# Graph attention, 16 batches on one core: two bodies per loop turn, another table of units for the next batch's transposes, and SyncE's loads by unit

## The chip, the cores and the metric

One NeuronCore of one Trainium2 chip runs the whole program. The metric is the device time of one execution in microseconds (us), the median of several runs. Lower is better.

## The reference

`x` is 16 batches of 1024 rows by 512 columns, `adj` a 1024 by 1024 matrix of zeros and ones, shared by all batches. Per batch:

```python
h = relu(layernorm(x))                        # over the 512 columns, eps 1e-5
q, k, v = h @ Wq + bq, h @ Wk + bk, h @ Wv + bv   # 8 heads of 64 columns
scores = q @ k.T / sqrt(64) + where(adj == 0, -1e9, 0)
x = x + softmax(scores) @ v
```

All of it is float32.

## The kernel before

**Engines.** TensorE (PE) multiplies and transposes. ScalarE (ACT) takes exponentials and evacuates PSUM into the rounded high parts of a number. VectorE (DVE) adds the mask with a running minimum and makes the low parts. GpSimd (POOL) normalises x, makes the low parts of k and v and finishes the output. SyncE (SP) issues every DMA. Each engine has a program of its own, written out by hand, and semaphores tie them together.

**Units.** A batch is 128 units (`UNITS`). There are 8 heads, each head has two groups of four blocks of 128 queries, and each group has 8 units, one per block of 128 keys. In unit u TensorE does, in `body`: `contract_hi` of unit u-2 (O += V times the high part of the transposed probabilities), `turn_probs` (four transposes of 128x128 probabilities into T, which has two banks), `contract_lo` of unit u-2 and, in even units, `score_ahead` (four score matmuls of 128x512 for a block five ahead). ScalarE copies T to `pT` (`probs_hi`), VectorE makes the rest (`probs_low`), and both go through the scores of every second unit (`exponential`, `shift`). In units 2, 10, 18, ... TensorE also turns the group's output back through the bank `misc` (`turn_out`), ScalarE copies it out (`copy_y`), and POOL adds it to x in three operations (`finish`).

**Fills.** All other work of TensorE is put behind certain units by tables, and all of it goes through the one PSUM bank `misc`:

- `QK_SLOTS`: the projections of q and k of the next pair of heads, in units 3, 4, 5, 6, 8, 9, 11 and 12 of each 32 (the last of them for the third pair is in unit 76).
- `V_SLOTS`: the projection of v, in units 121 to 127 and 0, 1.
- `HT_SLOTS`: `turn_h`, four transposes of one of the next batch's eight x tiles, in units 83, 85, 87, 88, 91, 92, 95 and 96. ScalarE makes the high part (`h_high`) in that unit, VectorE the low part (`h_low`) at the start of the next. POOL normalises tile t two units ahead of its slot (`NORM_AT`).
- `STATS_SLOTS`: `stats`, VectorE's mean and variance of the next batch's x tiles, in units 5, 7, 13, 37, 39, 45, 69 and 71.

The function `before` finds who used the bank `misc` last, and each user waits for that one's evacuation.

**SyncE.** x tiles come through `xln`, which holds two tiles (`XLN = 2`): tile t goes to place t % 2 as soon as the tile before it there is no longer needed. Each tile is loaded twice, once for the statistics and once to be normalised. SyncE's list for each quarter of a batch (a pair of heads p, 32 units) is: loads of x for the statistics; wait for the last pair's output, store it, wait for an earlier store and load the next residual (`xres`); copy half 0 of k (`copy_k`, which waits for `k_low`, POOL's low part); further loads for the statistics; copy half 1 of k; the next weights (`load_wqk`, 1 MB). In the third quarter tiles 0 and 1 are loaded between the two halves of k, and tiles 2 to 7 at the end, behind the weights:

```python
                        sp.wait_ge(qk_mm, 4 * (PAIRS * b + p + 1) + 4)
                        load_wqk((p + 2) % PAIRS)
                    if p == len(STATS_SLOTS) - 1 and not last:
                        for t in range(XLN, NB):
                            sp.wait_ge(h_turned, NB * (b + 1) + t - XLN + 1)
                            load_xln(b + 1, t)
```

SyncE takes its list in order, and a wait holds back all that stands behind it.

**The loop.** On each engine batch 0 and batch 15 are written out as they are, and batches 1 to 14 are one body in a loop (`Fori(1, B - 1)`), so each engine goes back to the top of its loop 13 times. The waits of the body count with the loop's register.

Of the kernel before, what the change touches and what calls it, by code (L numbers as in the profile page):

```python
# [34 lines left out]
B, N, D, H = 16, 1024, 512, 8  # L35
HD = D // H
C = D // P
NB = N // P
PAIRS = H // 2
GROUPS = 2 * H  # L40
GB = NB // 2
UNITS = GROUPS * NB
# [21 lines left out]
HIGH_AFTER = (1, 2)  # L64
LOW_AFTER = (1, 3)

HT_SLOTS = (83, 85, 87, 88, 91, 92, 95, 96)
HT_AT = {s: t for t, s in enumerate(HT_SLOTS)}
NORM_AT = {s - 2: t for t, s in enumerate(HT_SLOTS)}

STATS_SLOTS = ((5, 7, 13), (37, 39, 45), (69, 71))
STATS_AT = {s: t for t, s in enumerate(sum(STATS_SLOTS, ()))}
STATS_TILES = [[STATS_AT[s] for s in slots] for slots in STATS_SLOTS]


V_SLOTS = (121, 123, 124, 125, 126, 127)
# [4 lines left out]
XLN = 2  # L81
# [8 lines left out]
def adj_preln_kernel(nc, x, adj, Wq, bq, Wk, bk, Wv, bv, out):  # L90
    with ExitStack() as ctx:
# [3 lines left out]
        def sem(name):  # L95
            return ctx.enter_context(nc.semaphore(name))
# [66 lines left out]
        bn_done, mv_done, ln_part, ln_done = sem("bn_done"), sem("mv_done"), sem("ln_part"), sem("ln_done")  # L163
        h_turned, h_hi, h_lo = sem("h_turned"), sem("h_hi"), sem("h_lo")
# [47 lines left out]
        @block.sync  # L212
        def _(sp):
            def load_xln(b, t):

                sp.sem_inc(sp_passed)
                sp.dma_start(xln[:, t % XLN, :], x[b, t * P:(t + 1) * P, :]).then_inc(xln_in[t % XLN], 16)

            def load_xres(b, p):
                sp.sem_inc(sp_passed)  # L220
                src = x[b].rearrange("(i t) c -> t i c", t=P)[:, :, p * P:(p + 1) * P]
                sp.dma_start(xres[:, p % 2], src).then_inc(xres_in[p % 2], 16)

            def load_wqk(p):
                sp.dma_start(wqk[:].rearrange("p w c l n -> p (w c l n)").bitcast(F32),
                             wqk_dram[p]).then_inc(wqk_in, 16)

            def copy_k(b, p, half):

                cols = slice(half * HALF, (half + 1) * HALF)  # L230

                sp.wait_ge(k_low, 4 * (PAIRS * b + p) + 2 * (half + 1))
                for second in range(2):
                    _, k = qk_buffers(p, second)
                    own, other = (slice(0, HD), slice(HD, P))[::-1 if second else 1]
                    sp.dma_start(k[other, :, cols].bitcast(F32), k[own, :, cols].bitcast(F32)
                                 ).then_inc(k_copied, 16)

            def store(b, p):
                sp.sem_inc(sp_passed)  # L240
                dst = out[b].rearrange("(i t) c -> t i c", t=P)[:, :, p * P:(p + 1) * P]
                sp.dma_start(dst, xres[:, p % 2]).then_inc(stored[p % 2], 16)

            for w, src in enumerate((bq, bk)):
                sp.dma_start(bqk[:, w, :], src.rearrange("(r p) -> p r", p=P),
                             allow_slow_non_contiguous=True).then_inc(b_in, 16)
            sp.dma_start(bv_all[:], bv.partition_broadcast(P)).then_inc(b_in, 16)
            for i in range(4):
                src = x[0, 2 * i * P:(2 * i + 2) * P].rearrange("(t p) n -> p t n", p=P)
                sp.dma_start(x0[i // 2][:, 2 * (i % 2):2 * (i % 2) + 2], src).then_inc(x0_in[i], 16)  # L250
            for w, src in ((1, Wk), (0, Wq), (2, Wv)):
                sp.dma_start(stage[:, w], src.rearrange("(c p) n -> p c n", p=P)).then_inc(w_in[w], 16)

            adj_blocks = adj.rearrange("(i p) n -> p i n", p=P)

            def load_adj(i):
                sp.dma_start(probs[:, 2 * i:2 * i + 2, :], adj_blocks[:, 2 * i:2 * i + 2]).then_inc(adj_in[i], 16)

            sp.wait_ge(h_turned, GB)
            load_adj(3)  # L260
            for w in (1, 0):
                sp.wait_ge(w0_split, 2 - w)
                sp.wait_ge(wqk_split, (PAIRS - 1) * (2 - w))
                load_adj(w)
            sp.wait_ge(wv_split, 1)
            load_adj(2)

            def store_wqk(r):
                src = (wqk[:] if r == 0 else wqk_stage[:, r - 1]).rearrange("p w c l n -> p (w c l n)")
                sp.dma_start(wqk_dram[r], src.bitcast(F32)).then_inc(wqk_stored[r], 16)  # L270

            store_wqk(1)
            store_wqk(2)
            for half in range(2):
                copy_k(0, 0, half)
            store_wqk(3)
            store_wqk(0)
            sp.wait_ge(h_turned, NB)
            for t in range(XLN):
                load_xln(1, t)  # L280
            for p in range(2):
                load_xres(0, p)
            sp.wait_ge(qk_mm, 4)
            for r in range(PAIRS):
                sp.wait_ge(wqk_stored[r], 16)
            load_wqk(1)

            def body(b, first=False, last=False):
                for p in range(PAIRS):
                    if p < len(STATS_SLOTS) and not last:  # L290

                        for t in STATS_TILES[p][:2]:
                            if t < XLN and not first:
                                sp.wait_ge(h_turned, NB * (b + 1))
                            if t >= XLN:
                                sp.wait_ge(bn_done, NB * (b + 1) + t - XLN + 1)
                            if not (first and t < XLN):
                                load_xln(b + 1, t)
                    if not (first and p == 0):

                        sp.wait_ge(y_added, 4 * (PAIRS * b + p))
                        if p == 0:
                            store(b - 1, PAIRS - 1)
                        else:
                            store(b, p - 1)
                        if not (last and p == PAIRS - 1):
                            r = (p + 1) % 2

                            sp.wait_ge(stored[r], 16 * (2 * b + (p + 1) // 2))
                            if p == PAIRS - 1:  # L310
                                load_xres(b + 1, 0)
                            else:
                                load_xres(b, p + 1)
                    if not (last and p == PAIRS - 1):
                        copy_k(b, p + 1, 0)
                    if p < len(STATS_SLOTS) and not last:
                        for t in STATS_TILES[p][2:]:
                            sp.wait_ge(bn_done, NB * (b + 1) + t - XLN + 1)
                            load_xln(b + 1, t)
                    if p == len(STATS_SLOTS) - 1 and not last:  # L320

                        sp.wait_ge(bn_done, NB * (b + 2))
                        for t in range(XLN):
                            load_xln(b + 1, t)
                    if not (last and p == PAIRS - 1):
                        copy_k(b, p + 1, 1)
                    if not (last and p >= PAIRS - 2):

                        sp.wait_ge(qk_mm, 4 * (PAIRS * b + p + 1) + 4)
                        load_wqk((p + 2) % PAIRS)  # L330
                    if p == len(STATS_SLOTS) - 1 and not last:
                        for t in range(XLN, NB):
                            sp.wait_ge(h_turned, NB * (b + 1) + t - XLN + 1)
                            load_xln(b + 1, t)

            body(0, first=True)
            with sp.Fori(1, B - 1) as b:
                body(b)
            body(B - 1, last=True)
            sp.wait_ge(y_added, GROUPS * B)  # L340
            store(B - 1, PAIRS - 1)
            for r in range(2):
                sp.wait_ge(stored[r], 16 * B * PAIRS // 2)
# [3 lines left out]
        def _(gp):  # L347
# [100 lines left out]
                            finish(b, u // NB - 1)  # L448

            body(0, first=True)  # L450
            with gp.Fori(1, B - 1) as b:
                body(b)
            body(B - 1, last=True)
            finish(B - 1, GROUPS - 1)

# [2 lines left out]
        def _(pe):  # L458
# [151 lines left out]
                    fill(b, u, last)  # L610

            body(0, first=True)
            with pe.Fori(1, B - 1) as b:
                body(b)
            body(B - 1, last=True)
            for u in range(UNITS - LAG, UNITS):
                contract_hi(B - 1, u)
# [5 lines left out]
        def _(act):  # L623
# [127 lines left out]
                        h_high(b + 1, HT_AT[u])  # L751

            body(0, first=True)
            with act.Fori(1, B - 1) as b:
                body(b)
            body(B - 1, last=True)
            copy_out(B - 1, GROUPS - 1)
            copy_y(B - 1, GROUPS - 1)
# [3 lines left out]
        def _(dve):  # L762
# [119 lines left out]
                        stats(b + 1, STATS_AT[u])  # L882

            body(0, first=True)
            with dve.Fori(1, B - 1) as b:
                body(b)
            body(B - 1, last=True)
            invert(B - 1, GROUPS - 1)

# [18 lines left out]
```

## Time and profile before

| | |
|---|---|
| Median of 3 runs | 4150.72 us (4150.56 to 4152.28) |
| The profiled execution | 4145.39 us |
| Its span, first to last instruction | 4143.3 us |
| TensorE busy | 4075.5 us, 98% |
| ScalarE busy | 3142.6 us, 76% |
| VectorE busy | 3111.1 us, 75% |
| GpSimd busy | 1313.3 us, 32% |
| Mean share of the DMA engines | 22.2% (q1) |
| Granted TensorE clock | 0.999 of full speed |

Busy time is the union of an engine's instructions. The ends of matmuls are modelled, so a busy TensorE may still be issuing more slowly than it can. What a stretch costs is therefore read from the time between two starts, and a view of windows cut at the starts of `turn_probs` gives the length of a unit. In this text T82 is the start of the four transposes of unit 82.

### The profile page before, as it was taken

To read this page: it belongs to the slowest core of one execution; us is meant where nothing else is said; L and a number is where in the kernel's file an instruction comes from. 1 tells how busy PE (TensorE), PEld (TensorE's weight loads), DVE (VectorE), ACT (ScalarE), POOL (GpSimd) and SP (SyncE) were. 2 spreads that over 40 slices of the span, in tenths; PEclk is the share of its full clock that TensorE was granted. 3 is DMA by queue.
4 is the path that set the end of the run, shared out by engine and by line. 5 is a ranking of instruction groups with operands and counts; after the bars stand their busy time and mean duration, and the time that the engine had idled before them with its cause. 6 is when DMAs were issued, how large, how long until landed. Compare 5 with 4: busy or idle time off the path is not lost.

```text
span 4143.3 us, 77847 instructions
## 1 busy us (share of the span) xinstructions
PE 4075.5 (98%) x22528; PEld 3339.6 (81%) x22528; DVE 3111.1 (75%) x5128; ACT 3142.6 (76%) x5642; POOL 1313.3 (32%) x1665
## 2 busy tenths in 40 slices
PE   7999999999999999999999999999999999999999
PEld 6888888888888888888888888888888888888887
DVE  6877868778677786777767677786877768767687
ACT  5877868778687786877868688686886868868687
POOL 4333332333323333333333233332333333333222
PEclk9999999999999999999999999999999999999999
DMA  5221212212122221222212122121221212212111
GB/s 178 72 75 57 82 46 78 67 57 82 57 68 67 60 85 60 59 68 75 69 60 68 59 77 67 60 77 49 77 67 60 80 47 77 73 54 85 47 52 31
DMA packets 219597, 282.56 MB, mean 68 GB/s; under 512 B 12304, under 2 KB 143376, under 8 KB 210576
## 3 DMA queue, kind: packets, MB, share of 16 engines
q1 hardware_dynamic: 219152, 277.14, 22.2%
q8 instruction: 217, 3.56, 0.4%
q14 instruction: 228, 1.87, 0.1%
HBM read 172.23 MB, written 37.75 MB: 51 GB/s over the span
## 4 chain that ended last, share of the span: by engine, by line
PE 92%; ACT 2%; issue 2%; DMA 2%; POOL 1%; DVE 1%; SPq 0%; POOLq 0%; ACTq 0%; DVEq 0%
PE T L528 20%; PE misc L486 17%; PE S L516 11%; PE S L517 11%; PE O L540 10%; PE O L547 10%; PE misc L499 8%; PE misc L555 3%; DMA xln<-in_x 2%; PE misc L465 1%; ACT yparts L636 1%; ACT probs L653 1%; ACT pT L645 0%; DVE pT L811 0%; DVE bn L769 0%
## 5 line engine op out<-in xcount | busy, mean ns | idle before, releaser
L811 DVE TENSOR_TENSOR pT<-T,pT 128x512 fp32r<-128x512 f32 x2048 | 1401.5, 687 | 758.4 <-ACT pT L645 745.7
L645 ACT CAST pT<-T 128x512 fp32r<-128x512 f32 x2048 | 1189.0, 592 | 654.2 <-PE T L528 553.4
L805 DVE CUSTOM_DVE_ANT_0 S<-S,mask 128x1024 f32<-128x1024 f32 x1024 | 1257.4, 1228 | 10.0 <-issue 4.9
L528 PEld LDWEIGHTS T<-ident,probs 128*128 128x128 f32 x8192 | 1012.5, 140 | 270.1 <-ACT probs L653 14.1
L528 PE MATMUL T<-ident,probs 128*128 128x128 f32 x8192 | 1226.3, 272 | 3.7 <-DVE pT L811 2.9
L653 ACT ACTIVATE probs<-S,negmax 128x1024 f32<-128x1024 f32 x1024 | 1151.1, 1124 | 8.9 <-DVE negmax L805 5.8
L547 PE MATMUL O<-pT,vs 128*64 128x512 f32 x2048 | 975.6, 476 | 0.2 <-DVE pT L811 0.2
L540 PE MATMUL O<-pT,vs 128*128 128x512 f32 x2048 | 817.5, 399 | 14.0 <-issue 13.9
L486 PE MATMUL misc<-hT,wqk 128*128 128x512 f32 x3036 | 788.4, 395 | 8.1 <-ACT yparts L636 7.7
L486 PEld LDWEIGHTS misc<-hT,wqk 128*128 128x128 f32 x3036 | 557.0, 188 | 158.8 <-issue 25.7
L403 POOL TENSOR_TENSOR yparts<-yparts 128x256 f32<-128x256 f32 x256 | 188.3, 736 | 1112.4 <-ACT yparts L636 1112.4
L540 PEld LDWEIGHTS O<-pT,vs 128*128 128x128 f32 x2048 | 386.4, 189 | 69.8 <-issue 19.4
L516 PE MATMUL S<-kA,qA 128*128 128x512 f32 x1024 | 415.0, 405 | 4.0 <-ACT probs L653 3.1
L516 PE MATMUL S<-kB,qB 128*128 128x512 f32 x1024 | 414.9, 405 | 0.0
L517 PE MATMUL S<-kA,qA 128*128 128x512 f32 x1024 | 403.2, 394 | 0.0
L517 PE MATMUL S<-kB,qB 128*128 128x512 f32 x1024 | 402.0, 393 | 0.0
L499 PE MATMUL misc<-wv,hT 128*128 128x512 f32 x1476 | 360.9, 393 | 0.4 <-issue 0.4
L499 PEld LDWEIGHTS misc<-wv,hT 128*128 128x128 f32 x1476 | 273.6, 188 | 70.8 <-issue 10.2
L380 POOL TENSOR_TENSOR vs<-proj,vs 128x512 fp32r<-128x512 f32 x128 | 168.6, 1317 | 509.4 <-ACT vs L694 509.2
L393 POOL TENSOR_TENSOR kA<-proj,kA 64x512 fp32r<-64x512 f32 x128 | 165.9, 1296 | 511.4 <-ACT kB L679 511.4
L668 ACT ACTIVATE proj<-misc,bqk 128x512 f32<-128x512 f32 x253 | 174.2, 689 | 171.4 <-PE misc L486 171.4
L547 PEld LDWEIGHTS O<-pT,vs 128*64 128x64 f32 x2048 | 280.6, 137 | 0.8 <-DVE pT L811 0.7
(70 smaller groups left out, 3703.3 us busy)
## 6 DMA issues: line engine op xcount, KB each, us to landing
wqk<-wqk_split SPq DMA_DIRECT2D x63, 1024.0 KB, 7.0
xln<-in_x SPq DMA_DIRECT2D x240, 256.0 KB, 4.2
xres<-in_x SPq DMA_DIRECT2D x66, 512.0 KB, 3.7
kA<-kA SPq DMA_DIRECT2D x128, 256.0 KB, 3.2
kB<-kB SPq DMA_DIRECT2D x128, 256.0 KB, 3.8
out<-xres SPq DMA_DIRECT2D x64, 512.0 KB, 3.2
probs<-in_adj SPq DMA_DIRECT2D x4, 1024.0 KB, 4.9
wqk_split<-vs SPq DMA_DIRECT2D x3, 1024.0 KB, 10.5
```

Source lines behind the costliest of these rows:

```text
L403: gp.tensor_tensor(y, y, yparts[:, :, 1], ALU.add).then_inc(y_summed, 1)
L486: mm = pe.matmul(bank, wqk[:, w, c, wl, :], hT[:, hl, c, cols], start=n == 0, stop=n == len(parts) - 1)
L499: mm = pe.matmul(bank, hT[:, hl, c, j * P:(j + 1) * P], wv[:, wl, c, :], start=n == 0, stop=n == len(parts) - 1)
L516: pe.matmul(dst, q[:, i * P:(i + 1) * P], k[:, 0, cols], start=True, stop=False)
L517: mm = pe.matmul(dst, q[:, i * P:(i + 1) * P], k[:, 1, cols], start=False, stop=True)
L528: mm = pe.transpose(T[:, u % 2, i * P:(i + 1) * P], probs[:, (GB * g + i) % RING, j * P:(j + 1) * P], ident[:])
L540: pe.matmul(O[:], vs[:, j, head, :], pT[:, u % PT, 0, :], start=j == 0, stop=j == NB - 1)
L547: pe.matmul(O[:HD, :], vs[:, j, head, :HD], pT[:, u % PT, 1, :], start=False, stop=j == NB - 1, skip_group_check=j == NB - 1).then_inc(con ...
L645: act.copy(pT[:, u % PT, 0, :], T[:, u % 2, :]).then_inc(p_hi, 1)
L653: act.activation(probs[:, s % RING, :], S[:, s % 2, :], ACT.Exp, bias=negmax[:, s % RING:s % RING + 1], scale=-1.0, accum_out=rowsum[:, s ...
L805: dve.tensor_tensor_reduce(S[:, s % 2, :], S[:, s % 2, :], mask[:, s % NB, :], 1.0, 3.0e38, ALU.add, ALU.min, negmax[:, s % RING:s % RING ...
L811: dve.tensor_tensor(pT[:, u % PT, 1, :], T[:, u % 2, :], pT[:, u % PT, 0, :].bitcast(F32), ALU.subtract).then_inc(p_lo, 1)
```

## The change

1. The loop's turn holds two bodies on every engine: `Fori(0, B // 2 - 1)` with `body(2 * two + 1)` and `body(2 * two + 2)`. The loop then goes back 6 times.
2. `HT_SLOTS` becomes 77, 79, 83, 85, 88, 91, 94, 96.
3. `STATS_SLOTS` becomes 5, 7, 11, 13, 37, 39, 43, 45: the statistics of 69 and 71 move to 11 and 43.
4. SyncE's list is written by units. Each load of x stands at the unit of the step that frees its place, and the store, the copies of k and the weights at fixed units of each quarter (4, 8 and 15, 16).

```diff
-HT_SLOTS = (83, 85, 87, 88, 91, 92, 95, 96)
+HT_SLOTS = (77, 79, 83, 85, 88, 91, 94, 96)
...
-STATS_SLOTS = ((5, 7, 13), (37, 39, 45), (69, 71))
-STATS_AT = {s: t for t, s in enumerate(sum(STATS_SLOTS, ()))}
-STATS_TILES = [[STATS_AT[s] for s in slots] for slots in STATS_SLOTS]
+STATS_SLOTS = (5, 7, 11, 13, 37, 39, 43, 45)
+STATS_AT = {s: t for t, s in enumerate(STATS_SLOTS)}
+
+STORE_AT, COPY_K_AT, WQK_AT = 4, (8, 15), 16
...
             def body(b, first=False, last=False):
-                for p in range(PAIRS):
...
+                for u in range(UNITS):
+                    p, v = u // 32, u % 32
+                    if u == 0 and not first and not last:
+                        sp.wait_ge(h_turned, NB * (b + 1))
+                        for t in range(XLN):
+                            load_xln(b + 1, t)
+                    if v == STORE_AT and not (first and p == 0):
...
+                    if u in STATS_AT and not last:
+                        t = STATS_AT[u]
+                        sp.wait_ge(bn_done, NB * (b + 1) + t + 1)
+                        load_xln(b + 1, (t + XLN) % NB)
+                    for half in range(2):
+                        if v == COPY_K_AT[half] and not (last and p == PAIRS - 1):
+                            copy_k(b, p + 1, half)
+                    if u in HT_AT and HT_AT[u] + XLN < NB and not last:
+                        t = HT_AT[u]
+                        sp.wait_ge(h_turned, NB * (b + 1) + t + 1)
+                        load_xln(b + 1, t + XLN)
+                    if v == WQK_AT and not (last and p >= PAIRS - 2):
 
                         sp.wait_ge(qk_mm, 4 * (PAIRS * b + p + 1) + 4)
                         load_wqk((p + 2) % PAIRS)
...
             body(0, first=True)
-            with sp.Fori(1, B - 1) as b:
-                body(b)
+            with sp.Fori(0, B // 2 - 1) as two:
+                body(2 * two + 1)
+                body(2 * two + 2)
             body(B - 1, last=True)
```

The same edit of the loop stands on POOL, TensorE, ScalarE and VectorE.

**SyncE in the third quarter, before**, from the residual's load (L222) to the end of the quarter. `xln` is the place of the x tiles, `h_turned` counts the transposed tiles.

```order
L222 DMA xres<-in_x 128x8x128
L232 ISA
L236 DMA kA<-kA 64x2x512 [waits k_low]
L236 DMA kB<-kB 64x2x512
L322 ISA
L217 DMA xln<-in_x 128x512 [waits bn_done]
L217 DMA xln<-in_x 128x512
L232 REGISTER_ALU
L236 DMA kA<-kA 64x2x512 [waits k_low]
L236 DMA kB<-kB 64x2x512
L225 DMA wqk<-wqk_split 128x2048 [waits qk_mm]
L217 DMA xln<-in_x 128x512 [waits h_turned] x6
```

**The same place in the changed kernel.**

```order
L223 DMA xres<-in_x 128x8x128
L233 ISA
L237 DMA kA<-kA 64x2x512 [waits k_low]
L237 DMA kB<-kB 64x2x512
L218 DMA xln<-in_x 128x512 [waits h_turned]
L233 REGISTER_ALU
L237 DMA kA<-kA 64x2x512 [waits k_low]
L237 DMA kB<-kB 64x2x512
L218 DMA xln<-in_x 128x512 [waits h_turned]
L226 DMA wqk<-wqk_split 128x2048 [waits qk_mm]
L218 DMA xln<-in_x 128x512 [waits h_turned] x4
```

The two loads of tiles 0 and 1 have left the gap between the copies (they stand in the second quarter now), tile 2 has taken their place, tile 3 stands behind the second copy and ahead of the weights, and tiles 4 to 7 are behind the weights.

**VectorE in units 11 to 13 of the loop's body, before.** `probs_low` is `pT<-T,pT`, the statistics are `BN_STATS` and `BN_AGGR`.

```order
L787 TENSOR_TENSOR qA<-proj,qA 64x512
L810 REGISTER_ALU
L811 TENSOR_TENSOR pT<-T,pT 128x512
L810 REGISTER_ALU
L811 TENSOR_TENSOR pT<-T,pT 128x512
L803 REGISTER_ALU
L805 ISA S,negmax<-S,mask 128x1024
...
L811 TENSOR_TENSOR pT<-T,pT 128x512
L766 ISA
L769 BN_STATS bn<-xln 128x6
L770 REGISTER_ALU
L772 BN_AGGR mv<-bn 128x2
```

**The same units in the changed kernel.**

```order
L782 TENSOR_TENSOR qA<-proj,qA 64x512
L805 REGISTER_ALU
L806 TENSOR_TENSOR pT<-T,pT 128x512
L761 ISA
L764 BN_STATS bn<-xln 128x6
L765 REGISTER_ALU
L767 BN_AGGR mv<-bn 128x2
L805 REGISTER_ALU
L806 TENSOR_TENSOR pT<-T,pT 128x512
...
L806 TENSOR_TENSOR pT<-T,pT 128x512
L764 BN_STATS bn<-xln 128x6
L765 REGISTER_ALU
L767 BN_AGGR mv<-bn 128x2
```

Four instructions and the semaphore between them have come in behind the `probs_low` of unit 11, and all that follows on VectorE stands that much further from the loop's top.

## Rows read from the trace of the kernel before

**Rows 1.** The profile's first part: busy time (share of the span) xinstructions of each engine.

```profile
PE 4075.5 (98%) x22528; PEld 3339.6 (81%) x22528; DVE 3111.1 (75%) x5128; ACT 3142.6 (76%) x5642; POOL 1313.3 (32%) x1665
```

**Rows 2.** Who waited for whom: us in total, times, longest us.

```profile
PEld misc L486 <- ACT proj L668: 15.7, 56, 0.4
PE O L540 <- issue: 13.9, 13, 1.5
PE misc L465 <- POOL xln L374: 8.1, 11, 1.6
```

**Rows 3.** Windows on TensorE, T127 to T0 without a turn: length, busy (instructions), clock, DMA.

```profile
3910.67:3914.54 3.87, 3.87 (x20) 1.00 0.00 0
```

**Rows 4.** The same windows at the loop's 13 turns.

```profile
3139.94:3145.55 5.61, 4.13 (x19) 1.00 0.02 7
...
sum 67.45, PE 53.50; mean PE 4.12
```

**Rows 5.** Windows on TensorE, unit 77 (no fill) and unit 85, 15 batches each.

```profile
sum 13.50, PE 13.50; mean PE 0.90
...
sum 20.12, PE 20.12; mean PE 1.34
```

**Rows 6.** Windows on TensorE, unit 87, 15 batches.

```profile
2539.39:2542.51 3.12, 1.56 (x12) 1.00 0.11 41
...
3568.25:3569.70 1.45, 1.45 (x12) 1.00 0.31 119
...
sum 31.53, PE 23.27; mean PE 1.55
```

**Rows 7.** Timeline of SyncE, batch 3, T82 is 989.92: start, us, what.

```profile
990.50 0.60 SPq L236 DMA_DIRECT2D kA<-kA  x1
991.14 0.61 SPq L236 DMA_DIRECT2D kB<-kB  x1
991.80 0.66 SPq L225 DMA_DIRECT2D wqk<-wqk_split  x1
994.18 7.46 SPq L217 DMA_DIRECT2D xln<-in_x  x3
```

**Rows 8.** Timeline of POOL, the same stretch: [idle before <-releaser].

```profile
989.19 1.28 POOL L393 TENSOR_TENSOR kB<-proj,kB 64x512 fp32r<-64x512 f32 x1
995.64 0.78 POOL L374 TENSOR_SCALAR xln<-xln,negmean,rstd 128x512 f32<-128x512 f32 x1
999.68 1.53 POOL L374 TENSOR_SCALAR xln<-xln,negmean,rstd 128x512 f32<-128x512 f32 x2 [3.26 <-DMA xln<-in_x]
```

**Rows 9.** Timeline of TensorE, the same stretch: the fills of units 85, 87, 88.

```profile
996.61 0.60 PE L465 MATMUL misc<-ident,xln 128*128 128x128 f32 x4
1000.50 0.66 PE L465 MATMUL misc<-ident,xln 128*128 128x128 f32 x4 [0.57 <-POOL xln L374]
1002.83 0.60 PE L465 MATMUL misc<-ident,xln 128*128 128x128 f32 x4
```

**Rows 10.** DMA issues from 972 to 982, then from 994: KB, us to landing.

```profile
xln<-in_x SPq DMA_DIRECT2D x2, 256.0 KB, 4.0
...
xln<-in_x SPq DMA_DIRECT2D x1, 256.0 KB, 5.3
```

**Rows 11.** Timeline of VectorE, batch 3, units 11 to 15.

```profile
867.50 0.69 DVE L811 TENSOR_TENSOR pT<-T,pT 128x512 fp32r<-128x512 f32 x1 [1.00 <-ACT pT L645]
...
871.30 0.68 DVE L769 BATCH_NORM_STATS2 bn<-xln 128x6 f32<-128x512 f32 x1
872.51 0.18 DVE L772 BATCH_NORM_AGGREGATE mv<-bn 128x2 f32<-128x6 f32 x1 [0.53 <-DVE bn L769]
```

**Rows 12.** Windows on TensorE, batch 3, T13 to T17 and T45 to T49.

```profile
869.44:875.31 5.87, 5.65 (x34) 1.00 0.02 4
...
926.80:932.29 5.49, 5.49 (x33) 1.00 0.00 0
```

**Rows 13.** Groups of instructions of VectorE: the low part of a transposed tile.

```profile
L777 DVE SCALAR_TENSOR_TENSOR hT<-misc,hT 128x512 fp32r<-128x512 f32 x120 | 82.8, 690 | 18.0 <-ACT hT L684 17.9
```

More of the change, by code:

```diff
@@ L288, in body @@
             def body(b, first=False, last=False):
-                for p in range(PAIRS):
[L290 to L299, printed above, removed]
+                for u in range(UNITS):
[5 more added lines that the diff above has]
+                    if v == STORE_AT and not (first and p == 0):
                         sp.wait_ge(y_added, 4 * (PAIRS * b + p))
@@ L313, in body @@
                                 load_xres(b, p + 1)
[L314 to L327, printed above, removed]
+                    if u in STATS_AT and not last:
[10 more added lines that the diff above has]
+                    if v == WQK_AT and not (last and p >= PAIRS - 2):
                         sp.wait_ge(qk_mm, 4 * (PAIRS * b + p + 1) + 4)
                         load_wqk((p + 2) % PAIRS)
[L331 to L334, printed above, removed]
             body(0, first=True)
-            with sp.Fori(1, B - 1) as b:
-                body(b)
+            with sp.Fori(0, B // 2 - 1) as two:
+                body(2 * two + 1)
+                body(2 * two + 2)
             body(B - 1, last=True)
@@ L450, in _ @@
             body(0, first=True)
-            with gp.Fori(1, B - 1) as b:
-                body(b)
+            with gp.Fori(0, B // 2 - 1) as two:
+                body(2 * two + 1)
+                body(2 * two + 2)
             body(B - 1, last=True)
@@ L612, in _ @@
             body(0, first=True)
-            with pe.Fori(1, B - 1) as b:
-                body(b)
+            with pe.Fori(0, B // 2 - 1) as two:
+                body(2 * two + 1)
+                body(2 * two + 2)
             body(B - 1, last=True)
@@ L753, in _ @@
             body(0, first=True)
-            with act.Fori(1, B - 1) as b:
-                body(b)
+            with act.Fori(0, B // 2 - 1) as two:
+                body(2 * two + 1)
+                body(2 * two + 2)
             body(B - 1, last=True)
@@ L884, in _ @@
             body(0, first=True)
-            with dve.Fori(1, B - 1) as b:
-                body(b)
+            with dve.Fori(0, B // 2 - 1) as two:
+                body(2 * two + 1)
+                body(2 * two + 2)
             body(B - 1, last=True)
```

## The prediction

> **What bounds the kernel now.** I read the profile's first part, then who waited for whom, then windows cut at the starts of TensorE's probability transposes, and last the timelines around the two places where such windows were too long. TensorE is busy for 98% of the span [rows 1], so only two things can shorten the run: TensorE's idle time, or a slower issue of its work. No matmul is added or removed. The waits name two places. TensorE sat idle 13 times, 13.9 us in all, ahead of the first product with V of a body (L540) with "issue" as the cause, which means that nothing in the trace held it [rows 2]; 13 is the number of times that the loop goes back. And it waited 8.1 us for normalised x tiles [rows 2]. The windows give the whole price of both, since they also count what TensorE lost beside its idle time.
>
> **The turn of the loop.** From unit 127 to unit 0 TensorE takes 3.87 us where the program simply runs on, here from batch 14 into the written-out batch 15 [rows 3]. At the 13 turns it takes 67.45 / 13 = 5.19 us [rows 4]. The instructions are the same, so a turn costs 1.32 us. Before there are 13 turns, after there are 6 (seven trips of two bodies). Seven turns fewer: 7 x 1.32 = **-9.2 us**. The lower end of the gain is what remains if the six turns left get dearer (a rival below); the upper end is 13 x 1.32 = 17.2 us, if they became free, for which nothing speaks.
>
> A rule speaks against a gain of this size, and the trace decides against it. The Trainium skill, "Advanced Engine Details and Errata", section "Control Flow Timing", puts a compare-and-branch at about 108 ns. By that figure alone, as an estimate, this term would be 7 x 0.108 = 0.8 us. The Trainium skill, "Runtime: NRT & Kernel Launch", section "Instruction fetch mechanics", says that a taken branch out of the loaded code forces a fetch before execution goes on; the 1.32 us agree with that rule and not with the bare branch.
>
> **The wait at unit 87.** A unit with a transposing fill and no score takes 20.12 / 15 = 1.34 us (unit 85), one without a fill 0.90 us, so a fill costs 0.44 us [rows 5]. Unit 87 has the same work as unit 85, but takes 31.53 / 15 = 2.10 us, between 1.45 and 3.12 us [rows 6]. It loses 0.76 us per batch, 11.4 us in all. The timelines tell why. SyncE issues the second half of the k copies at 990.50 and 991.14, the 1 MB of weights at 991.80 and tile 2 at 994.18, as soon as tile 0 is transposed [rows 7]. The tile lands 5.3 us after its issue, where two like it, issued without weights ahead of them, took 4.0 us [rows 10]. POOL sat idle for 3.26 us until it landed, normalised from 999.68 on [rows 8], and TensorE's fill began at 1000.50 after 0.57 us idle [rows 9]. In the change tile 2 is freed by unit 77 and needed in unit 83, its load stands ahead of the k copies, and six units lie between. This wait goes: **-11.4 us**.
>
> **What can take its place.** Here the moved steps count, each with the queue that it is moved past.
>
> *Tile 3, unit 85.* Its load stands behind the second half of k, and is issued where the weights were. The k copies are issued when POOL has made the low part (its operation ended at 989.19 + 1.28 = 990.47 [rows 8]), which is 0.58 us behind T82. That part hangs on ScalarE's work of unit 78. The fill in unit 79 lies between and moves T82 back by 0.44 us, so the copies go out at T82 + 0.14, tile 3 at T82 + 0.14 + 0.64 + 0.7 = T82 + 1.5, and it lands 4.0 us later [rows 10] at T82 + 5.5. POOL is free for it at 995.64 = T82 + 5.72, after the output's three operations, needs 0.78 us and is done at T82 + 6.5 [rows 8]. The fill of unit 85 starts at 996.61 = T82 + 6.69 [rows 9]. The margin is 0.2 us, and landings spread by more than that: unit 87's length ran from 1.45 to 3.12 us [rows 6]. Ends: 0 and the 11.4 us of now. I take 0.2 us per batch, near the low end, because the nearest row has the tile ahead of the weights: **+3.0 us**.
>
> *Tile 4, unit 88.* It is issued at the same place as tile 2 was, 994.18 = T82 + 4.26, with the weights ahead and now tile 3 ahead of them too. A quarter of the weights' size adds at most some 0.7 us, so it lands by T82 + 10.3 and is normalised by T82 + 11.3. The fill of unit 88 started at 1002.83, 12.9 us behind T82; without unit 87's fill and its wait of 0.8 us in this batch that is T82 + 11.7. A margin of 0.4 us: I take **+0.8 us**, ends 0 and 7 us.
>
> *Unit 77.* Its fill comes right behind the last projection, and must wait until ScalarE has evacuated the bank. The nearest rows are units 5 and 37, where a projection follows another's evacuation: the weight loads wait 15.7 us in 56 cases there, 0.28 us each [rows 2], part of it behind running matmuls. Ends 0 and 15 x 0.28 = 4.2 us. I take 0.1 us each: **+1.5 us**.
>
> *VectorE and ScalarE behind units 77 and 79.* A fill gives TensorE 0.44 us of work but VectorE 0.69 us [rows 13]. These two now come in a stretch where both engines still have the projection's parts to finish. Two times 0.25 us per batch is the upper end, 7.5 us; 0 is the lower, since the packed units 87, 88, 91, 92, 95 and 96 carry the same load now and outside of unit 87 I find no loss of this kind. I take 0.1 us per batch, **+1.5 us**.
>
> *The statistics.* Those of units 69 and 71 go to 11 and 43. Behind the `probs_low` of unit 11 VectorE idles 1.00 us [rows 11], and mean and variance take 0.68 and 0.18 us with a short pause between. They fit but for a tenth, and half a us of idle time follows ahead of unit 13's. Their x tile is loaded behind the store of unit 4, over five units ahead. Zero, ends 0 and 15 x 0.4 = 6 us.
>
> There is a stall that may go. In unit 13 VectorE pauses 0.53 us between the two instructions of the statistics, with nothing to wait for but the first [rows 11], and units 13 to 16 take 5.87 us against 5.49 for units 45 to 48, which hold the same work [rows 12]. That is 0.38 us in 14 batches, 5.3 us. The same instructions don't pause in unit 45, so it is tied to a place in VectorE's code, and all that stands there shifts by the statistics of unit 11. It can move into an idle stretch (-5.3), stay (0), or turn up elsewhere. I take **-3.0 us**.
>
> SyncE's other steps only move by a few units, and nobody waits for the store or the residual. POOL's and SyncE's programs get longer, not fuller.
>
> **Sum.** -9.2 - 11.4 + 3.0 + 0.8 + 1.5 + 1.5 - 3.0 = -16.8 us. The sum is made against the profiled execution, 4145.4 us, which would become 4128.6. That execution is 5.3 us below the median of the runs shown; taken off that median the change gives 4150.7 - 16.8 = **4133.9 us**.
>
> A change of under 0.2% (8.3 us) can hardly be told from none here, so "faster" means below 4142.4 us.
>
> **The rivals.**
>
> *The load's wait only moves.* Tile 3 stands behind two copies of k and tile 4 behind the weights. If the landings come 0.6 us later than reckoned, units 85 and 88 together lose what 87 loses now. For it: the margins are 0.2 and 0.4 us. Against it: both places have more room than unit 87 had. The sum is then -16.8 + (11.4 - 3.8) = -9.2, so 4141 us; with a stall of unit 13 that stays, 4144. Chance 0.16.
>
> *The six turns left get dearer.* The bodies are twice as long on all five engines, so POOL and SyncE too may have to load code at a turn. For it: their bodies are short now. Against it: TensorE's body is far longer than any other already, and POOL is busy for 32% only [rows 1]. If a turn costs twice as much, the six give back 7.9 us: 4142 us. Chance 0.11. The Trainium skill, "Runtime: NRT & Kernel Launch", section "Instruction fetch mechanics", speaks of a window of two pages of code, which POOL's doubled body might leave; the trace shows no turn of that kind.
>
> *A turn is a bare branch, and the 1.32 us are the start of a body.* Then nothing is gained there: -16.8 + 9.2 = -7.6, 4143 us. Against it: the last body, entered without a turn, takes 3.87 us and no more [rows 3]. Chance 0.03. The Trainium skill's figure for a branch, in the section on control flow above, stands behind this rival.
>
> *VectorE becomes the bound (slower).* Each of eight fills brings it 0.25 us more than it brings TensorE. It decides once VectorE has no idle time left in these units. Then all eight cost 0.25 us in 15 batches, 30 us, in place of the 1.5 us above: 4162 us. For it: the eight now begin in units where the projection's rest still runs. Against it: they are spread over 20 units instead of 14. Chance 0.05.
>
> **Chances.** The forecast (4125 to 4140 us) has 0.62, the rivals 0.35, and 0.03 is left for what I don't see. Faster: the forecast, and about 0.13 of the rivals and the rest, 0.75. Same: 0.18. Slower: 0.07. The range takes in the unknown terms downward (unit 13's stall gone, no new waits: 4125) and the first three rivals upward: 4125 to 4146 us.
>
> **What would show it.** Windows from T127 to T0: nine of 15 at 3.87 us and six at about 5.2. The wait at unit 83 zero; units 85 and 88 at most 0.2 us too long on average. Units 13 to 16 near 5.5 us in place of 5.87. From T76 to T100 the unit lengths add up to some 0.4 us less per batch than now. I am wrong if units 85 and 88 lose as much as 87 did, if the six turns cost clearly more than 1.3 us each, or if VectorE pauses in new places in the plain units.

## The result, and the profile of the changed kernel

The changed kernel takes **4124.58 us** (median of 4 runs, 4122.22 to 4125.00), the kernel before took 4150.64 us beside it. The ratio is 0.9935, with a 95% interval of 0.9918 to 0.9952. That is 26.1 us less, where 16.8 were forecast. The range began at 4125 us, so the time lies 0.4 us below it.

The profiled execution took 4122.22 us. The first part of its profile, beside [rows 1]:

```profile
PE 4069.9 (99%) x22528; PEld 3339.3 (81%) x22528; DVE 3112.2 (76%) x5128; ACT 3137.9 (76%) x5642; POOL 1311.5 (32%) x1665
```

The work is the same to the instruction. The waits that answer to [rows 2] (engine, tile, line, who held it: us in total, times, longest):

```profile
PEld misc L479 <- ACT proj L662: 15.7, 56, 0.4
PE O L533 <- issue: 5.9, 6, 1.3
PEld misc L458 <- ACT proj L662: 3.4, 14, 0.2
PE misc L458 <- POOL xln L366: 1.7, 3, 0.8
```

The idle time at the head of a body has gone from 13 cases to 6, and TensorE waits for a normalised tile 3 times in place of 11. A new entry is the fill of unit 77 (L458), held by ScalarE's evacuation.

Windows on TensorE from T127 to T0, beside [rows 3, 4]: from batch 2 to 3 (a turn), 3 to 4 (within a turn's two bodies), and the sum of all 15.

```profile
824.05:829.23 5.18, 4.10 (x20) 1.00 0.04 11
1080.11:1083.95 3.84, 3.84 (x19) 1.00 0.00 0
...
sum 65.30, PE 59.40; mean PE 3.96
```

Before, the 15 added up to 67.45 + 2 x 3.87 = 75.19 us.

Windows of unit 87, 15 batches, beside [rows 6]; it has no fill any more:

```profile
sum 13.52, PE 13.52; mean PE 0.90
```

Windows of unit 85, beside [rows 5]: batch 4, batches 5, 7 and 11, and the sum.

```profile
1247.07:1248.41 1.34, 1.34 (x11) 1.00 0.94 344
1502.48:1504.60 2.12, 1.55 (x11) 1.00 0.81 317
...
2013.28:2015.61 2.33, 1.56 (x11) 1.00 0.79 306
...
3035.03:3036.97 1.94, 1.56 (x11) 1.00 0.91 354
...
sum 22.73, PE 21.00; mean PE 1.40
```

Windows of unit 77 and of unit 88, 15 batches each. A unit with a fill and no score takes 1.34 us if nothing holds it [rows 5]; unit 88, with a fill and a score, took 34.04 us in all before.

```profile
sum 21.60, PE 21.60; mean PE 1.44
...
sum 34.02, PE 34.02; mean PE 2.27
```

Windows T13 to T17 of batch 3, beside [rows 12]:

```profile
865.30:870.78 5.48, 5.48 (x33) 1.00 0.22 56
```

So the difference of the two spans, 4143.3 - 4120.4 = 22.9 us, lies in three places but for half a us:

| Stretch, all batches | before | after | difference |
|---|---|---|---|
| T127 to T0, 15 times | 75.19 | 65.30 | -9.9 |
| T76 to T100, 15 times | 632.98 | 625.60 | -7.4 |
| T13 to T17, 14 looped batches | 81.90 | 76.83 | -5.1 |

The rest is unit 54 (27.80 us in all before, 27.41 after), where two batches of the kernel before took 2.10 and 1.98 us in place of 1.82, and unit 104 (48.08 and 47.77).

### The profile page after: what moved, and what is told of

The parts are those of the page before. It is cut to its first block, busy times and chain, and to the rows that moved or that the text cites. A ratio compares the mean times of both kernels' runs of the same rounds, so it can differ in the third digit from the quotient of the medians.

```text
span 4120.4 us, 77658 instructions
## 1 busy us (share of the span) xinstructions
PE 4069.9 (99%) x22528; PEld 3339.3 (81%) x22528; DVE 3112.2 (76%) x5128; ACT 3137.9 (76%) x5642; POOL 1311.5 (32%) x1665
## 4 chain that ended last, share of the span: by engine, by line
PE 94%; ACT 2%; issue 2%; POOL 1%; DMA 0%; DVE 0%; SPq 0%; POOLq 0%; ACTq 0%; DVEq 0%
PE T L521 21%; PE misc L479 17%; PE S L509 11%; PE S L510 11%; PE O L540 11%; PE O L533 11%; PE misc L492 8%; PE misc L548 3%; PE misc L458 1%; ACT yparts L630 1%; ACT probs L647 1%; DMA xln<-in_x 0%; POOL vs L417 0%; ACT pT L639 0%; POOL xln L366 0%
```

## The experiments

Every kernel ran beside the kernel before. The windows of the profiled executions are the finer measure: a stretch that has no wait repeats within 0.1 us (T13 to T17 adds up to 76.83 us in the changed kernel and to 76.78 in its repetition), while whole executions of the kernel before spread from 4141.6 to 4153.6 us in one series. Four of the kernels below (VectorE's code moved by 5 and by 123, TensorE's code moved, tile 3 ahead) ran once each, so for them only the windows count.

### Two bodies per turn alone

```diff
-            with sp.Fori(1, B - 1) as b:
-                body(b)
+            with sp.Fori(0, B // 2 - 1) as two:
+                body(2 * two + 1)
+                body(2 * two + 2)
```

(the same on the other four engines)

> The kernel before with the two bodies per turn alone. Theory (the turn itself costs): the 7 turns that go are worth 7 x 1.3 = 9 us, so about 4141 to 4142 us; windows from T127 to T0 are 3.86 us in nine batches and about 5.2 in six; unit 87 still takes 2.1 us and units 13 to 16 still 5.87 us, since their tables have not moved. Rival (the longer bodies make a turn dearer): the six turns take 6 us or more and the gain is under 3 us.

4137.58 us against 4148.96, ratio 0.9973 (0.9962 to 0.9984). T127 to T0 adds up to:

```profile
sum 64.65, PE 59.40; mean PE 3.96
```

That is 10.5 us less than before. Unit 87 keeps its wait (33.18 us in all, 31.53 before). T13 to T17, batch 3 (first body of a turn) and batch 4 (second body):

```profile
868.80:874.69 5.89, 5.65 (x33) 1.00 0.02 4
1125.36:1130.86 5.50, 5.50 (x34) 1.00 0.00 1
```

The seven turns that went were worth 1.5 us each, the six that stay take 5.0 us each, and the rival of dearer turns falls. The second body was not expected to lose its pause. By the trace it stands 637 instructions of VectorE behind the first, which is no multiple of 128 (the experiments with moved code show why that counts). T13 to T17 in the 14 looped batches adds up to 79.44 us in place of 81.90, so 2.5 us of this kernel's gain are not the turns'.

### The statistics alone

```diff
-STATS_SLOTS = ((5, 7, 13), (37, 39, 45), (69, 71))
+STATS_SLOTS = ((5, 7, 11, 13), (37, 39, 43, 45), ())
```

> The kernel before with the statistics in units 5, 7, 11, 13, 37, 39, 43, 45 alone, SyncE's list as it was. Theory (VectorE's pause of unit 13 is tied to a place in its code, which the instructions of unit 11 push away): units 13 to 16 fall from 5.87 to 5.5 us in each looped batch, 5 us in all, about 4145.5 us; nothing else moves. Rival (the pause is cleared by the loads coming by units): no change, 4150.6 us, and units 13 to 16 stay at 5.87 us.

4143.24 us against 4148.96, ratio 0.9990 (0.9981 to 1.0000). T13 to T17 in the 14 looped batches adds up to 76.83 us in place of 81.90, 5.1 us less, as in the changed kernel. As expected.

### The transposes' table alone, with SyncE's list as it was

```diff
-HT_SLOTS = (83, 85, 87, 88, 91, 92, 95, 96)
+HT_SLOTS = (77, 79, 83, 85, 88, 91, 94, 96)
```

> The kernel before with x tiles transposed in units 77, 79, 83, 85, 88, 91, 94, 96 and SyncE's list as it was, that is with tile 2 behind the weights. Theory (what counts is which transfer stands ahead of the tile): tile 2 is issued after the weights at T82 + 2.8, lands 7 us after T82 + 2.1 and is ready near T82 + 10, while its fill in unit 83 wants it at T82 + 3.5: some 6 us lost per batch, 15 x 6 = 90 us, about 4240 us, all of it in unit 83. Rival (the spacing of the slots alone takes the wait away): 11 us faster, 4139 us.

4287.43 us, ratio 1.0333 (1.0313 to 1.0354): slower, and by more than expected. Batch 4, T82 is 1287.65. SyncE, POOL, and TensorE's fill of unit 83:

```profile
1289.06 0.66 SPq L225 DMA_DIRECT2D wqk<-wqk_split  x1
1289.89 2.49 SPq L217 DMA_DIRECT2D xln<-in_x  x2
```

```profile
1298.85 0.77 POOL L374 TENSOR_SCALAR xln<-xln,negmean,rstd 128x512 f32<-128x512 f32 x1 [11.12 <-DMA xln<-in_x]
```

```profile
1299.68 1.11 PE L465 MATMUL misc<-ident,xln 128*128 128x128 f32 x4 [8.71 <-POOL xln L374]
1300.44 0.78 PE L540 MATMUL O<-pT,vs 128*128 128x512 f32 x1
```

Tile 2 was issued at T82 + 2.24, half a us earlier than reckoned, but landed 8.7 us after its issue, at T82 + 10.9 and not T82 + 9.1: the weights themselves took 8.9 us there against a median of 7.0. Unit 83 takes 157.54 us in all, 132 more than before. And unit 84 behind it takes 3.12 us on average (2.72 to 3.42), where it takes 1.83 in the changed kernel with the same matmuls. Unit 84 in batches 0 and 4:

```profile
234.75:238.16 3.41, 3.41 (x11) 0.50 0.27 77
...
1301.02:1304.10 3.08, 3.08 (x12) 0.57 0.34 85
```

The granted clock is 0.50 in the first of these windows, the lower of its two levels (1.2 GHz), and 0.57 on average in the second; over the whole run it falls from 0.999 to 0.983. What TensorE had done before was to stand still for 8.71 us. The lower clock costs 19.4 us in unit 84 alone, which the expectation had not counted. The wait for tile 2's load, which stands behind the weights, and this clock make the kernel 138 us slower; the table of slots is worth nothing without the list.

### SyncE's list by units alone

The edit is the new body of SyncE with the old tables, `STATS_SLOTS` flat.

> SyncE's list by units with the old tables of slots and one body per turn. Theory (with the old slots tile 2 is freed in unit 83 and stands behind the weights in either list): unit 87 keeps its 2.1 us, no change, 4150 us within 3. Rival (the list is what removes the wait at 87): 4139 us.

4147.37 us against 4148.96, ratio 0.9997 (0.9987 to 1.0006): no difference. Unit 87 takes 31.85 us in all (31.53 before). The list alone is worth nothing either.

### VectorE's code moved by five instructions

```diff
+            for _ in range(5):
+                dve.sem_inc(padded)
             with dve.Fori(1, B - 1) as b:
```

> The kernel before with five semaphore increments on VectorE ahead of its loop, which do nothing but move the loop's code by five instructions. Theory (the pause of unit 13 is a border in VectorE's code): units 13 to 16 go from 5.87 to 5.5 us in the looped batches, 5 us in all, as with the statistics moved. Rival (the statistics of unit 11 cleared the pause by doing work earlier): 5.87 us stays.

4142.30 us against one run of before at 4143.19; the 5 us do not show in one execution of each. T13 to T17, 14 looped batches:

```profile
sum 76.83, PE 76.83; mean PE 5.49
```

The same 76.83 us as with the statistics moved, from five instructions that do nothing. The pause belongs to a place in the code. There are more such places. 256 instructions behind unit 13's pause, counted in the trace, VectorE pauses ahead of a running minimum in the kernel before (batch 3, first line), and does not with the code moved (second line). There it pauses 123 instructions behind the old place of unit 13's, which is 128 behind the new one (third line):

```profile
963.14 1.23 DVE L805 CUSTOM_DVE_ANT_0 S<-S,mask 128x1024 f32<-128x1024 f32 x1 [0.35 <-issue]
```

```profile
963.97 1.23 DVE L806 CUSTOM_DVE_ANT_0 S<-S,mask 128x1024 f32<-128x1024 f32 x1
...
918.57 0.69 DVE L812 TENSOR_TENSOR pT<-T,pT 128x512 fp32r<-128x512 f32 x1 [0.27 <-issue]
```

### The changed kernel with VectorE's code moved by 123

> The changed kernel with 123 semaphore increments on VectorE ahead of its loop: five less than 128. Theory (a border every 128 instructions, and the statistics of unit 11 brought five): the border lands between the two instructions of unit 13's statistics again in the first body of a turn and units 13 to 16 take 5.87 us there; in the second body it lies two instructions off, as in the two bodies alone, and they keep 5.5 us. That is 7 x 0.36 = 2.5 us. Rival (no period of 128): both bodies stay at 5.5 us.

4138.99 us. 10.7 us of this are the 123 increments themselves, which VectorE works off once at the head of batch 1 (T1 to T2 takes 14.35 us there and 3.64 in the other batches). T13 to T17, batches 3 and 4:

```profile
878.81:884.68 5.87, 5.64 (x33) 1.00 0.16 51
1133.77:1139.27 5.50, 5.50 (x34) 1.00 0.20 53
```

The pause is back in the first body and not in the second, 79.41 us in all, 2.6 more. (The other 3.5 us of this one execution lie in unit 0, +1.6, and in single waits.) Five instructions move it away and 128 bring it back, and the other pauses of the experiment before stand 256 and 128 instructions behind a place of this one. So a border comes every 128 instructions on VectorE.

### The changed kernel with TensorE's code moved by 160

> The changed kernel with 160 semaphore increments on TensorE ahead of its loop, so that its code is fetched some 13 us earlier in each body. Theory (in batches 3, 5, 7 and 11 a fetch of TensorE's code at T82 + 1 to 3 us holds up the transfer of tile 3): the fetches fall outside of T82 to T82 + 6 and unit 85 takes 1.34 us in every batch, 2.6 us less in all. Rival (the longer waits of those batches have another cause, as the k copies' own spread): unit 85 still takes 1.6 to 2.3 us in several batches.

4151.99 us, of which 22.3 us are the increments, worked off ahead of batch 1 (T127 to T0 takes 26.16 us there). Unit 85, batches 4, 5 and 6:

```profile
1274.03:1276.13 2.10, 1.56 (x11) 1.00 0.91 359
1530.80:1532.15 1.35, 1.35 (x12) 1.00 0.92 331
1785.25:1787.84 2.59, 1.55 (x11) 1.00 0.80 326
...
sum 25.40, PE 21.88; mean PE 1.46
```

The expectation missed, and what the rival said would be seen is what came: unit 85 still takes 1.5 to 2.6 us in eight batches. The fetches had not left the 6 us from T82 on. The waits moved from the odd batches to the even ones all the same, although only TensorE's code had moved, which speaks for the fetch and against a spread of the copies' own. The DMA view of the 6 us from T82 on says it in packets. Changed kernel, batch 4 (unit 85 takes 1.34 us):

```profile
kB<-kB SPq DMA_DIRECT2D x1, 256.0 KB, 3.8
```

Changed kernel, batch 5 (2.12 us), the same 6 us; q8 is the queue that carries code:

```profile
q8 instruction: 1, 0.02, 1.0%
...
kB<-kB SPq DMA_DIRECT2D x1, 256.0 KB, 5.2
```

With the code moved, batch 6 (2.59 us):

```profile
q8 instruction: 1, 0.02, 1.0%
...
kB<-kB SPq DMA_DIRECT2D x1, 256.0 KB, 5.7
```

and batch 5 there has no q8 packet in that stretch, a k copy of 3.8 us and a unit 85 of 1.35 us. One packet of 16 KB of code in the wrong 6 us makes the k copy land 1.4 to 1.9 us later, and tile 3 behind it. The packet takes 1.0% of 16 engines in 6 us, which is 0.96 us of one of them. Tile 3's landing in the changed kernel, from its issue, batch 4 and batch 5:

```profile
xln<-in_x SPq DMA_DIRECT2D x1, 256.0 KB, 3.6
...
xln<-in_x SPq DMA_DIRECT2D x1, 256.0 KB, 4.8
```

The packets and the long units go together in the traces. In the changed kernel a q8 packet starts in these 6 us in batches 3, 5, 7 and 11, and these are the four with a long unit 85. In its repetition it is batches 3, 5, 7, 9 and 13, again exactly the long ones. With TensorE's code moved it is seven of the eight long ones, and no short one; batch 13, with 1.54 us, has none. With seven bodies it is three of the longer ones, and batches 7 (1.73 us) and 14 (1.51 us) have none. And with VectorE's code moved by 123 one packet, at T82 + 0.92 in batch 3, makes no long unit. So the fetch is the main cause of these waits, and not the only one.

In batch 5 of the changed kernel POOL shows it (timeline, T82 is 1496.47):

```profile
1503.05 0.77 POOL L366 TENSOR_SCALAR xln<-xln,negmean,rstd 128x512 f32<-128x512 f32 x1 [0.84 <-DMA xln<-in_x]
```

and in batch 4, with T82 at 1241.05, it waits for nothing and starts at T82 + 5.72 behind the output's operations:

```profile
1246.77 0.77 POOL L366 TENSOR_SCALAR xln<-xln,negmean,rstd 128x512 f32<-128x512 f32 x1
```

### Tile 3 ahead of the k copies

```diff
-STORE_AT, COPY_K_AT, WQK_AT = 4, (8, 15), 16
+STORE_AT, COPY_K_AT, WQK_AT = 4, (8, 16), 16
```

> The changed kernel with the second half of the k copies one unit later in SyncE's list (unit 16 in place of 15 of each quarter), so that tile 3 is issued ahead of the copies at about T80 in place of T82 + 1.5. Theory (unit 85's wait is tile 3 behind the copies): unit 85 takes 1.34 us in every batch, 2.6 us less, and unit 88 stays at 2.27 us. Rival (POOL's order of work sets unit 85): it stays at 1.52 us on average.

4122.78 us (4122.22 for the changed kernel's profiled execution). Unit 85 takes 20.11 us in all, 1.34 in each batch, so its wait is gone (-2.6 us), although the fetches still fall there in six batches. But the expectation had unit 88 unchanged, and unit 88 takes 35.09 us in all, 1.1 more, nearly all of it in batches 5 and 7:

```profile
1507.62:1510.11 2.49, 2.49 (x16) 1.00 0.03 10
...
2018.01:2021.01 3.00, 2.50 (x16) 1.00 0.03 11
```

Tile 4 still stands behind the weights, and in batch 7 POOL is idle for 5.03 us until it lands. T76 to T100 adds up to 624.12 us in place of 625.60: a gain of 1.5 us, too little for a whole execution to show.

### The changed kernel again, seven bodies, even slots, and all three

> The changed kernel itself once more, beside the others on one chip. Both theories: about 4124 us, 23 to 26 us below the kernel before, with nine windows from T127 to T0 of 3.86 us and six of 4.8 to 5.4.

> The changed kernel with seven bodies per turn, so that each engine goes back once. Theory (each turn costs 1.3 us whatever the body's length): five turns less are worth 6.5 us, about 4118 us; one window from T127 to T0 of about 5.2 us and fourteen of 3.86. Rival (a turn gets dearer with the body's length): the one turn takes 7 us or more. Pauses of VectorE and ScalarE at borders of their code may turn up in other units, each at 0.4 us.

> The changed kernel with the x tiles transposed in units 78, 80, 84, 86, 88, 92, 94, 96: all even, so that the scores of the unit stand between the last user of the bank and the fill. Theory (a fill in the odd unit right behind the output's transposes waits 0.35 us for the evacuation, and the one of unit 77 waits 0.1 us): units 83 and 91 lose their 0.35 us and 77 its 0.1 us, 15 x 0.8 = 12 us, about 4112 us. Rival (VectorE and ScalarE are the bound in these units, and a fill beside the scores' unit makes them later): what is won at 83 and 91 is lost in the units behind, 4124 us.

> Seven bodies per turn, the even slots and tile 3 ahead of the k copies together. Theory (the terms add): 6.5 + 12 + 2 = 20 us below the changed kernel, about 4104 us. Rival: the terms overlap and it stays above 4112 us.

The edits against the changed kernel:

```diff
-            with sp.Fori(0, B // 2 - 1) as two:
-                body(2 * two + 1)
-                body(2 * two + 2)
+            with sp.Fori(0, 2) as seven:
+                for i in range(7):
+                    body(7 * seven + 1 + i)
...
-HT_SLOTS = (77, 79, 83, 85, 88, 91, 94, 96)
+HT_SLOTS = (78, 80, 84, 86, 88, 92, 94, 96)
```

The third kernel has both and tile 3 ahead of the k copies.

| Kernel | us | ratio to before (95%) | T127 to T0 | T76 to T100 |
|---|---|---|---|---|
| changed, again | 4124.78 | 0.9940 (0.9924 to 0.9957) | 65.09 | 627.83 |
| seven bodies | 4118.51 | 0.9927 (0.9910 to 0.9943) | 58.88 | 626.62 |
| even slots | 4106.24 | 0.9895 (0.9878 to 0.9911) | 65.53 | 610.44 |
| all three | 4101.25 | 0.9886 (0.9869 to 0.9902) | 59.42 | 610.42 |

The one turn of the seven bodies:

```profile
2097.36:2102.41 5.05, 4.11 (x20) 1.00 0.04 10
```

This turn costs 1.2 us, and five turns less are worth 6.2 us. The one turn of the third kernel takes 5.42 us, so 1.6; single turns of the kernel before cost 1.0 to 1.7 us (windows of 4.84 to 5.61 us), and a body seven times as long is inside that. The pause of unit 13 is back in the third body of each turn of seven (5.84 and 5.83 us in batches 3 and 10), which fits: two bodies are 1274 instructions, 6 short of a multiple of 128, and the statistics had moved the code by 5.

The repeated changed kernel has longer waits at unit 85 than the first time (24.29 us in all, +4.2 and not +2.6), which is most of its 627.83 against 625.60. The even slots gain more than expected: 15.2 us in T76 to T100 against the first changed kernel and 17.4 against its repetition, where 12 were expected. Units 83, 91, 77 and 85, none of which has a fill now, take 0.90 to 0.91 us, and the fills in the even units 78, 84 and 92 cost their bare 0.44 us:

```profile
sum 34.06, PE 34.06; mean PE 2.27
```

(unit 78, 15 batches). The 0.35 us of a fill right behind the output's transposes are gone in both places, as are the 0.10 us of unit 77 and the 2.6 to 4.2 us of unit 85, whose tile now has until unit 86. VectorE and ScalarE have not become a bound. All three together take 23.5 us off the changed kernel, 20 were expected; this is the fastest kernel of the study.

## Why the prediction was off, point by point

- **The turn.** Forecast -9.2 us, measured -9.9 (and -10.5 for the two bodies alone). Right in mechanism and near in size: 1.3 us per turn for one body, 1.1 to 1.3 for two, and 1.2 and 1.6 for the two single turns of seven.
- **The wait at unit 87.** Forecast -11.4 us, measured 31.53 us less the 13.52 of a unit without and 15 x 0.44 of its fill: -11.4. Right. The two experiments with the table alone and the list alone show that neither half of the edit does it.
- **Tile 3 at unit 85.** Forecast +3.0, measured 22.73 - 20.12 = +2.6 us, and +4.2 in the repetition. The issues came as reckoned, to 0.1 us (k copy issued at T82 + 0.10 in batch 4, tile 3 at T82 + 1.52); the landing took 3.6 us there in place of 4.0. What I called the spread of landings has a cause that I had not seen: for the most part a fetch of TensorE's code between them.
- **Tile 4 at unit 88.** Forecast +0.8, measured 0. It took 5.3 us to land in batch 4, as long as tile 2 did before; the 0.7 us that I had added for tile 3 ahead of it stand in no row and did not come.
- **Unit 77.** Forecast +1.5, measured 21.60 - 20.12 = +1.5 us.
- **VectorE and ScalarE behind units 77 and 79.** Forecast +1.5, measured 0: unit 79 takes 1.34 us. The fills in the even slots confirm that these engines have room there.
- **The stall of unit 13.** Forecast -3.0, measured -5.1. **Of the terms of the sum this is the one that was mis-sized most.** I saw that the pause was tied to a place in the code, and still took a mean of "gone" and "stays" in place of counting. The listing would have settled it: the new statistics put five instructions ahead, the border stays where it is, and it then lies ahead of unit 13's `probs_low`, where VectorE idled half a us anyway. The two bodies alone had already cleared it in the second body, which the prediction did not see either.
- **The profiled execution and the median. This is the step that put the time outside of the range.** I took the sum, worked out on the profiled execution, off the median one to one. By the profiled executions the change is 4145.39 - 4122.22 = 23.2 us, by the medians 26.1, and 24.2 in the second series: the profiled execution of before was 5.3 us below its median, that of after 2.4. With 23.2 us off the median the time would have been 4127.5 us, inside the range; the step is off by 2.9 us. Why the executions of before lie further above the profiled one is open. The runs give a hint: the kernels with the old table of transposes spread by 7 to 12 us in series of 7 to 23 executions, the changed kernel and its three successors by 1.3 to 3.6 (4 executions each; but the 4 executions of the kernel before beside the result lay within 1.9, too). Unit 87, which runs from 1.45 to 3.12 us with its wait, keeps that wait in all of the former and has none in the latter. No trace was taken of an execution of before that lies above its median, so this is not shown.

The miss is 26.1 - 16.8 = 9.3 us. The sum of the terms as measured is -9.9 - 11.4 + 2.6 + 1.5 - 5.1 = -22.3 us, 5.5 beyond the forecast. Four fifths of that are the stall of unit 13 (2.1) and two small costs that did not come (1.5 and 0.8). Another 0.9 are places outside of the terms and the difference of span and time, and 2.9 the step from the profiled execution to the median. The lower end of the range was worked out as "the stall gone, no new waits", 4125 us. The stall did go, but new waits of 4.1 us came (units 85 and 77), so the terms alone give no time below the range. The mechanisms of the two large terms were right. None of the rivals came in: the turns did not get dearer, the load's wait moved in part and not in full, and VectorE did not become the bound.

## What to carry to other kernels

Cut windows at a repeated instruction and compare the same window with and without the suspected cost: that priced the loop's turn and the late tile to within a us before anything ran. The sum then holds for executions like the profiled one; the median can move by some us more or less. A table of slots and the list of the queue that feeds them are one edit: either alone was worth nothing, or cost 3%. With the bound engine 98% busy there were still 48 us to be had, from how often the loop turns, from which transfer stands ahead of which, and from keeping two users of a PSUM bank a score's time apart.

## What the runs showed of the hardware

- **A turn of the loop costs TensorE 1.1 to 1.6 us, with no sign that the length of the body counts.** The means are 1.32 us (13 turns of one batch), 1.26, 1.24 and 1.14 (6 turns of two) and 1.2 and 1.6 (single turns of seven); a batch is 3200 of TensorE's instructions. What fills this time no run shows.
- **A border every 128 instructions of VectorE's code makes a pause of about 0.37 us.** Five instructions of padding moved it, 123 brought it back in the changed kernel, and two more pauses stand 256 and 128 instructions behind a place of this one. A body has 642 instructions on VectorE and so five borders; one of them cost the run time, the others showed no loss in TensorE's units. The Trainium skill, "Runtime: NRT & Kernel Launch", section "Instruction fetch mechanics", says that the crossing of a border in the code is mostly hidden. The runs agree with "mostly", and show 5.1 us where it was not. The same section puts a border at every 256 instructions; on VectorE the runs show 128.
- **A fetch of TensorE's code delays the data that share the DMA engines with it.** With one packet of 16 KB, 1% of the engines' time in 6 us, beside it a 256 KB copy took 5.2 to 5.7 us in place of 3.8, and the delay moved to other batches when the code moved.
- **After a stall of 8.7 us TensorE came back at a lower clock**: the next unit took 3.12 us on average in place of 1.83, with a granted clock of 0.50 to 0.65.
